# Deformable convolution, attention and 32-expert MLP on one core: three routing groups, two of them inside the last image's steps, and identity products on TensorE

## The chip, the cores and the metric

The kernel runs on one core of a Trainium2 chip. The metric is the device time of one execution in microseconds (us). TensorE (PE) multiplies matrices out of SBUF into PSUM, VectorE (DVE), ScalarE (ACT) and GpSimd (POOL) compute elementwise, and SyncE (SP) issues most of the DMA transfers. Each engine runs its own instructions in order and waits on semaphores.

## The reference

Eight images of 32 x 32 positions with 64 channels go through three stages, each with a residual addition.

```python
x = x + deform_conv(group_norm(x), kernel, bias, offset_w, offset_b)   # 3x3, offsets by a second 3x3 conv
t = to_tokens(x)                                                     # (8, 1024, 64)
t = t + causal_attention(layer_norm(t), Wq, bq, Wk, bk, Wv, bv)        # one head of 64
y = layer_norm(t)
logits = y @ gate_w.T + gate_b                                        # (8, 1024, 32)
probs = softmax(logits, axis=1)                                       # over the tokens
topv, topi = top_k(probs, 8)                                          # each expert takes 8 tokens
pooled = einsum("bked,bke->bed", y[topi], topv)                       # one vector for each image and expert
h = gelu([pooled, 1] @ weight1[e])                                    # 65 x 256, exact gelu
o = [h, 1] @ weight2[e]                                               # 257 x 64
t[topi] += o * topv                                                   # scattered back to the chosen tokens
```

## The kernel before

Tokens stand as 8 tiles of 128 for each image (`tok`). The program has four blocks, with a barrier between each two: `convolve_and_attend`, `route`, `mlp` and `combine`.

**The first block** works through the eight images in a pipeline. For each engine a table (`PE_AT`, `ACT_AT`, `DVE_AT`, `POOL_AT`, `SP_AT`) gives every step of an image a place in the engine's order, and image b is shifted by b times `STEPS`; only the order follows from these numbers, the time is set by semaphores. Images 0, 6 and 7 have tables of their own, images 1 to 5 share one. The steps that matter here:

- *prepare*: PE turns the image to channels (`turn`, L452), ACT and DVE copy it (`raw`, L463, L465), PE sums over groups (`groups`, L503), POOL normalises (`normalise`), PE convolves for the offsets (`offsets`, L553, L560), ACT evicts them (`leave`, L573), DVE and ACT make the interpolation weights ("tents"), which SP writes to DRAM (`near`) and reads back spread over partitions (`stage`, L826; `load`), three pieces deep.
- *convolve*: eight pieces an image. PE multiplies rows with the kernel (`mix`, L1215), ACT copies them (`rows`, L876), ACT finishes the column weights of a piece once its `stage` transfer has landed (`columns`, L866, L869), DVE multiplies weights (`weights`, L1073), PE forms the result in 16 `pair` steps (L1248) and turns it back (`back`).
- *attend*: layer norm, query and key (`query`, `key`), eight score rows with maximum (L1035), exponential (L961), transposes (L1105), values (L1117), output (`out`, L1204), second layer norm, channels (L1125, L914), gate (L1195), and the logits go to ACT's `rows4` (L970) and by four DMAs (L813) to the 128 rows of their half of the images. The choice for the first four images (softmax, top eight, mask in `pm`) runs in DVE steps inside image 7's table (`DVE_CHOICE`).

If some offset is too large, the block's end branches to a slow path (`unless_near`); it isn't taken with these inputs.

**route** asks for the expert weights, makes the choice for images 4 to 7 (`Choice`, L1574 to L1597), and for each half turns the mask (L1662), copies it (L1646) and gathers by 32 products (L1671: for each of 4 images and 8 tiles, two images side by side), which leaves `lhs`. **mlp** does 32 products of layer one (L1704, bias as a 65th row, four experts side by side in the array), gelu, transposes (L1711), layer two (L1719), bias (L1746), a product with a selection matrix that puts results behind their images (L1728), and four copies (L1752). **combine** multiplies with the mask in eight pieces (L1785), adds to the tokens (L1795) and stores each piece by two DMAs (L1777).

## Time and profile before

| | |
|---|---|
| runs | 508.09, 507.71, 504.94 us |
| median | 507.71 us |
| profiled execution | 507.9 us, its span 506.1 us |
| TensorE, busy | 416.1 us (82% of the span) |
| VectorE, busy | 345.3 us (68%) |
| ScalarE, busy | 289.8 us (57%) |
| GpSimd, busy | 159.5 us (32%) |
| mean granted clock of TensorE | 0.897 |
| HBM | 64.74 MB read, 7.01 MB written |

The times are those of whole executions. The busy times are from one profiled execution and overlap each other. A granted clock of 1.00 is 2.4 GHz, 0.50 is 1.2 GHz.

### The profile page before, as it was taken

The page shows a single profiled execution, that of the slowest core. Times are in us where ns is not written, and L with a number is a line of the kernel's source. Part 1 is how long each engine was busy: PE and PEld are TensorE (multiplying, and loading weights), DVE is VectorE, ACT ScalarE, POOL GpSimd, SP SyncE. Part 2 cuts the span into 40 slices and gives each one's busy share as a digit, 9 for nine tenths or more (in the row PEclk, how much of TensorE's full clock was granted, in tenths as well). Part 3 has the DMA queues.
Part 4 walks back from the last instruction along what each step waited for, and adds up shares of the span by engine and source line. Part 5 has one row for each costly group of instructions (what it writes and reads, how often), then busy time and mean ns, then how long its engine had stood idle before and what let it go on. Part 6 is the DMA issues. An engine that isn't in the chain of part 4 may idle for free. (4 is left out here: it accounts for less than half of the span.)

```text
span 506.1 us, 14009 instructions
## 1 busy us (share of the span) xinstructions
PE 416.1 (82%) x5845; PEld 307.5 (61%) x5845; DVE 345.3 (68%) x478; ACT 289.8 (57%) x531; POOL 159.5 (32%) x119
## 2 busy tenths in 40 slices
PE   1606985899999999999999999999999788227574
PEld 0204572576777677767767776767867556226274
DVE  3234668777898889889889989888896653213034
ACT  2323264778787687778677776877676456022100
POOL 2006007106534535472354446040640430310000
PEclk9756597999999999999999999999999969755589
DMA  9598969788787778588867789868730000039208
GB/s 221 97 208 189 222 144 231 179 205 177 188 205 177 177 183 186 123 207 195 186 160 174 175 176 207 198 158 198 181 71 12 2 2 12 1 70 229 84 3 166
DMA packets 33698, 75.61 MB, mean 149 GB/s; under 512 B 22365, under 2 KB 25373, under 8 KB 27293
## 3 DMA queue, kind: packets, MB, share of 16 engines
q1 hardware_dynamic: 28750, 72.68, 62.7%
q10 hardware_dynamic: 4880, 1.98, 1.7%
q8 instruction: 48, 0.79, 0.7%
q14 instruction: 20, 0.16, 0.1%
HBM read 64.74 MB, written 7.01 MB: 142 GB/s over the span
## 5 line engine op out<-in xcount | busy, mean ns | idle before, releaser
L1073 DVE TENSOR_TENSOR wring<-stage 96x640 f32<-96x640 f32 x192 | 173.0, 943 | 32.5 <-ACT stage L869 28.5
L1248 PE MATMUL psum<-wring,zring 96*64 96x160 f32 (+4 forms) x1728 | 124.8, 293 | 6.4 <-DVE wring L1073 6.4
L1248 PEld LDWEIGHTS psum<-wring,zring 96*64 96x64 f32 x1728 | 104.6, 141 | 20.9 <-issue 15.9
L1035 DVE TENSOR_REDUCE negmax<-psum 128x1 f32<-128x128 f32 (+3 forms) x64 | 48.3, 754 | 34.5 <-PE psum L1097 34.4
L1215 PE MATMUL psum<-kern,img 64*32 64x192 f32 x1536 | 58.5, 343 | 9.0 <-ACT zring L876 8.4
L876 ACT ACTIVATE zring<-psum 96x768 f32<-96x768 f32 x64 | 51.4, 803 | 23.0 <-PE psum L1215 21.4
L902 ACT ACTIVATE pT<-psum 128x512 f32<-128x512 f32 (+2 forms) x96 | 46.0, 483 | 28.4 <-PE psum L1105 28.1
L961 ACT ACTIVATE prob<-psum,negmax 128x128 f32<-128x128 f32 (+3 forms) x64 | 47.0, 734 | 22.9 <-DVE negmax L1035 18.4
L1093 PE MATMUL psum<-kT,qT 64*128 64x128 f32 (+4 forms) x400 | 51.7, 361 | 4.6 <-DVE kT L1030 1.5
L1105 PE MATMUL psum<-const,prob 128*128 128x128 f32 x288 | 50.5, 287 | 3.2 <-ACT pT L902 3.0
L866 ACT ACTIVATE stage<-stage,const 96x384 f32<-96x384 f32 x64 | 38.9, 608 | 20.5 <-DMA stage<-near 20.3
L1215 PEld LDWEIGHTS psum<-kern,img 64*32 64x32 f32 x1536 | 29.8, 110 | 25.1 <-ACT zring L876 12.0
L1093 PEld LDWEIGHTS psum<-kT,qT 64*128 64x128 f32 x400 | 33.5, 195 | 18.6 <-issue 9.7
L522 POOL TENSOR_SCALAR gs<-gs 64x1 f32<-64x1 f32 (+1 forms) x8 | 7.4, 927 | 114.1 <-DVE gs L514 114.1
L1117 PE MATMUL psum<-pT,ln 128*64 128x128 f32 x576 | 42.3, 278 | 0.7 <-ACT pT L902 0.7
L1105 PEld LDWEIGHTS psum<-const,prob 128*128 128x128 f32 x288 | 31.9, 144 | 13.8 <-issue 8.0
L1117 PEld LDWEIGHTS psum<-pT,ln 128*64 128x64 f32 x576 | 35.4, 137 | 6.3 <-issue 3.7
L1543 POOL TENSOR_TENSOR rn_tmp<-tok,rn_small 128x512 f32<-128x512 f32 x8 | 11.2, 1402 | 87.4 <-DVE rn_small L1529 87.4
L869 ACT ACTIVATE stage<-stage 96x384 f32<-96x384 f32 x64 | 33.5, 523 | 2.0
L527 POOL TENSOR_SCALAR img<-img,gs 64x1024 f32<-64x1024 f32 x7 | 28.2, 4022 | 0.8
L1543 POOL TENSOR_TENSOR an_tmp<-tok,an_small 128x512 f32<-128x512 f32 x8 | 10.0, 1251 | 47.5 <-DVE an_small L1529 47.5
L582 DVE TENSOR_TENSOR tents<-offT,const 128x1536 f32<-128x1536 f32 x8 | 15.4, 1930 | 9.0 <-ACT offT L573 9.0
(120 smaller groups left out, 525.9 us busy)
## 6 DMA issues: line engine op xcount, KB each, us to landing
stage<-near SPq DMA_DIRECT2D x192, 288.0 KB, 5.5
w<-in_w SPq DMA_DIRECT2D x1, 2080.0 KB
tok<-in_x SPq DMA_DIRECT2D x8, 256.0 KB, 5.2
images<-img SPq DMA_DIRECT2D x8, 256.0 KB, 3.8
w<-in_w SPq DMA_DIRECT2D x1, 2048.0 KB
img<-img SPq DMA_DIRECT2D x7, 256.0 KB, 3.0
near<-tents SPq DMA_DIRECT2D x32, 45.0 KB
shifts<-offT SPq DMA_DIRECT2D x8, 128.0 KB, 6.4
```

The costliest lines, as they stand in the source:

```text
L866: act.activation(dx, dx, ACT.Abs, bias=cst("negx")[0:KX, 0:1]).then_inc(f["abs"], 1)
L869: act.activation(dx, dx, ACT.Relu, bias=1.0, scale=-1.0).then_inc(f["tx"], 1)
L876: act.activation(zring[0:KX, q % ZRING].rearrange("p (s e) f -> p e s f", e=2), psum[0:KX, 0:2, 0:2 * K * C].rearrange("p e (s f) -> p e s ...
L902: act.activation(pT[:, t % DEEP, j * P:(j + nb) * P], psum[:, prob_bank(n, a), 0:nb * P], ACT.Copy).then_inc(s["pe"], 1)
L961: act.activation(prob[:, t % 2, 0:(t + 1) * P].rearrange("p (h k) -> p h k", k=row_half(t)), score_rows(t, a), ACT.Exp, bias=negmax[:, t:t ...
L1035: dve.tensor_reduce(negmax[:, t:t + 1], score_rows(t, a), AX.XY, ALU.max, negate=True).then_inc(s["mx"], 1)
L1073: dve.tensor_tensor(rows[:, ky, :, place], stage[0:KX, q % STG, ky, 1:, :], stage[0:KX, q % STG, ky, 0, :].unsqueeze(1).to_broadcast([KX, ...
L1093: ins = pe.matmul(psum[:, bank, c * n:c * n + n], qT[C * h:C * h + C, t * P:(t + 1) * P], kT[C * h:C * h + C, first:first + n], start=True ...
L1105: ins = pe.transpose(psum[:, prob_bank(n, a), m * P:(m + 1) * P], prob[:, t % 2, (j + m) * P:(j + m + 1) * P], ident)
L1117: ins = pe.matmul(psum[C * h:C * h + C, 7, t // 2 * P:(t // 2 + 1) * P], normed(a)[:, j, :], pT[:, (t + h) % DEEP, j * P:(j + 1) * P], sta ...
L1215: ins = pe.matmul(psum[W * kx:W * kx + W, e, n * K * C:(n + 1) * K * C], img[C * e:C * e + C, b % 2, row, :], kern[C * e:C * e + C, kx, :] ...
L1248: ins = pe.matmul(psum[C * e:C * e + C, 2 + half, (lo % 16) * W:(lo % 16 + n) * W], zring[0:KX, q % ZRING, i % 2 * 2 + e, ky * C:(ky + 1) ...
```

## The change

Everything now stands in one block, `run_all`, without the three barriers. The images form three routing groups, `GROUPS = ((0, 4), (4, 6), (6, 8))`.

- The choice, turning and gathering of groups 0 and 1 (`choose`, `pooled`), and layer one, gelu and transposes of their experts (`many`), are steps in image 7's table. Their SBUF places overlay tiles that the convolution and the attention no longer need: `hidden` and `hiddenT` lie in `pT`, `outs` in `prob`, the third mask in `qT`.
- The expert weights are asked for by a step `weights` in image 7's table on SP, behind the last convolution.
- The last image's logits go directly to their rows of the third group, without a DMA.
- Behind the tables each engine has an end (`pe_end`, `act_end`, `dve_end`), where group 2 (images 6 and 7) gets its choice, gather, experts, weighting and stores, while groups 0 and 1 are moved, weighted and stored in between.
- Layer one takes its bias on DVE (`add_bias`) and puts eight experts side by side, in both halves of the rows. The gather takes one image at a time, with half of the experts on each half of the output rows: 8 tiles x 2 products an image.
- `stay_awake` has PE multiply the identity by itself into a bank that nobody reads: 16 products behind image 0's turn, and 8, 6 and 5 products in `pe_end`.
- All five order tables are new, `STEPS` is 1120.

```diff
-STEPS, ROUND = 944, 4881
+STEPS, ROUND = 1120, 4577
 PE_AT = (      # image 7, the rows that are new
+        pooled=[5889, 6865, 10417, 11042, 13729, 14081],
+        many=[14497, 17361, 17473, 17985, 22001]))
 ACT_AT = (     # image 0
-        columns=[145, 225, 226, 305, 385, 465, 706, 753],
-        rows=[-1583, -287, 81, 257, 497, 705, 737, 929],
+        columns=[-2431, -191, 753, 1185, 1234, 1505, 1729, 1811],
+        rows=[-3535, -1007, -687, 929, 1233, 1521, 1809, 1812],
...
+        if step == 0 and g == 0:
+            pe.wait_ge(f["both"], 2 * B - 1)
+        if step == 0 and g == 1:
+            pe.wait_ge(pooled[0].s_pT, run + 1)
+        if step < 2:
+            pooled[g].turn(pe, step, 2, run)
+        else:
+            pooled[g].gather(pe, 2, run)
...
+        def pe_end(pe):
+
+            many.layer2(pe, 0)
+            stay_awake(pe, 3, 8)
+            many.move(pe, 1)
+            stay_awake(pe, 3, 6)
+            for n in range(3):
+                pe_weigh(pe, n)
+            stay_awake(pe, 3, 5)
+            pooled[2].turn(pe, 0, 0)
+            pe_weigh(pe, 3)
+            pooled[2].gather(pe, 1)
+            for n in range(4, 6):
+                pe_weigh(pe, n)
+            pe.wait_ge(pooled[2].s_pT, 1)
+            single.layer1(pe)
+            for n in range(6, len(strips)):
+                pe_weigh(pe, n)
+            pe.wait_ge(s_x, len(strips))
+            for n in range(4):
+                single.turn(pe, n)
+            single.layer2(pe, 0)
+            single.move(pe, 1)
...
+            act.activation(spare[:, 1:2], ident[:, 0:1], ACT.Exp)
+            choices[2].exponentials(act)
+            act.wait_ge(s_zero, 2)
+            many.keep(act, 1, copy)
+            act.activation(spare[:, 2:3], ident[:, 0:1], ACT.Gelu)
+            pooled[2].keep_turned(act, 0, 0)
+            pooled[2].keep(act, 1)
+            for n in range(4):
+                single.gelu(act, n)
+            for n in (2, 3):
+                single.keep_turned(act, n, copy)
+            store_last(act, 1)
...
+            dve_choose(dve, 2, 0)
+            dve.wait_ge(s["pt"], ONE + B * NCK)
+            many.keep_out(dve, 0)
+            for step in range(1, 5):
+                dve_choose(dve, 2, step)
+            for n in range(len(strips)):
+                dve_add(dve, n)
+            for n in range(4):
+                single.add_bias(dve, n)
+            for n in range(2):
+                single.keep_turned(dve, n, dve.tensor_copy)
+            single.keep_out(dve, 0)
+            single.keep(dve, 1, dve.tensor_copy)
...
+        def stay_awake(pe, bank, count):
+
+            for n in range(count):
+                pe.matmul(psum[:, bank, 0:P], ident, ident, start=True, stop=True)
...
             if n in at["turn"]:
                 bank_free(pe, in_z, b, n, True)
                 prep.to_channels(pe, b)
+                if b == 0:
+                    stay_awake(pe, 7, 16)
...
                 for b, at in in_order(SP_AT):
+                    if at in table(SP_AT, b)["weights"]:
+                        sync.wait_ge(f["mm"], 2 * NG4)
+                        sync.wait_ge(f["w_ok"], K * NG4)
+                        load_weights(sync)
...
+    def gather(self, pe, bank, run=0):
+        half = E // 2
+        pe.wait_ge(self.s_tT, self.parts * (run + 1))
+        for u in range(self.count):
+            for t in range(NT):
+                for r in range(2):
+                    ins = pe.matmul(self.psum[C * r:C * r + C, bank, half * u:half * u + half],
+                                    self.ln2[:, self.first + u, t, :],
+                                    self.taken[:, t, E * u + half * r:E * u + half * r + half],
+                                    start=(t == 0), stop=(t == NT - 1))
+        ins.then_inc(self.s_po, 1)
...
+    def layer1(self, pe, run=0):
+        for i in range(4):
+            for j in range(4):
+                for r in range(2):
+                    ins = pe.matmul(self.psum[E * j:E * j + E, 2 * r + i // 2, i % 2 * HID:(i % 2 + 1) * HID],
+                                    self.lhs[C * r:C * r + C, 4 * i + j, :], self.w1[C * r:C * r + C, 4 * i + j, :],
+                                    start=True, stop=True)
+            if i % 2:
+                ins.then_inc(self.s["h"], 1)
```

ScalarE at the start, from the eviction of image 0's offsets to the raw copy of image 1. `near` to `stage` transfers are what `f_stage0` and `f_stage1` wait for; before:

```order
L573 ACTIVATE offT<-psum,ob 128x256 [waits p_off_mm]
L876 ACTIVATE zring<-psum 96x2x2x192 [waits f_z_mm]
L593 ACTIVATE tents<-tents 128x2x640 [waits p_t_raw]
L596 ACTIVATE tents<-tents 128x2x640 [waits p_t_abs]
L876 ACTIVATE zring<-psum 96x2x2x192 [waits f_z_mm] x2
L463 ACTIVATE img<-psum 64x4x128 [waits p_x_t]
L866 ACTIVATE stage<-stage,const 96x3x128 [waits f_stage0]
```

and now (`memory` holds `stage`, `wring` and `zring`):

```order
L587 ACTIVATE offT<-psum,ob 128x256 [waits p_off_mm]
L607 ACTIVATE tents<-tents 128x2x640 [waits p_t_raw]
L610 ACTIVATE tents<-tents 128x2x640 [waits p_t_abs]
L935 ACTIVATE memory<-psum 96x2x2x192 [waits f_z_mm]
L925 ACTIVATE memory<-memory,const 96x3x128 [waits f_stage0]
L928 ACTIVATE memory<-memory 96x3x128 [waits f_abs]
L935 ACTIVATE memory<-psum 96x2x2x192 [waits f_z_mm] x2
L925 ACTIVATE memory<-memory,const 96x3x128 [waits f_stage1]
L928 ACTIVATE memory<-memory 96x3x128 [waits f_abs]
L477 ACTIVATE img<-psum 64x4x128 [waits p_x_t]
```

The second and third row copies and the raw copy of image 1 moved behind the first and second column steps.

TensorE at the end of the program, from the second group's turn to the move of the results; before:

```order
L1662 MATMUL psum<-const,pm 128x128 [waits r1_tk]
L1671 MATMUL psum<-takenT,ln 64x32 [waits r_tT]
L1615 UNCONDITIONAL_BRANCH
L1698 UNCONDITIONAL_BRANCH [waits barrier_Pool_Activation_PE_DVE_SP_release]
L1704 MATMUL psum<-w,lhs 32x256 [waits s_w]
...
L1719 MATMUL psum<-w,hT 32x64 [waits e_hT]
L1728 MATMUL psum<-outs,pick 128x64 [waits e_out]
```

and now, from the second expert layer of groups 0 and 1 (`ea`) to the first expert layer of group 2 (`r2`, `eb`); L1391 is `stay_awake`, L1224 the weighting:

```order
L2028 MATMUL psum<-memory,pT 32x64 [waits ea_hT]
L1391 MATMUL psum<-const 128x128 x8
L2045 MATMUL psum<-prob,memory 128x64 [waits ea_out]
L1391 MATMUL psum<-const 128x128 x6
L1224 MATMUL psum<-memory,chosen 128x256 [waits c_lg_sb,ea_kept]
L1224 MATMUL psum<-memory,chosen 128x256 x5
L1391 MATMUL psum<-const 128x128 x5
L1936 MATMUL psum<-const,qT 128x64 [waits r2_tT,r2_step]
L1224 MATMUL psum<-memory,chosen 128x256 x2
L1952 MATMUL psum<-memory,ln 64x16 [waits r2_tT]
L1224 MATMUL psum<-memory,chosen 128x128 [waits e_x]
L1980 MATMUL psum<-memory 32x256 [waits r2_pT]
```

Work of groups 0 and 1 moved ahead of and between the steps of group 2.

## Rows read from the trace of the kernel before

**Rows 1.** The page: the span, and TensorE's granted clock in 40 slices

```profile
span 506.1 us, 14009 instructions
...
PEclk9756597999999999999999999999999969755589
```

**Rows 2.** Windows, by stage: length, busy us of each engine, clock, DMA share, GB/s

```profile
100.00:350.00 250.00, 244.70 (x3725) 183.85 (x3725) 219.56 (x298) 188.60 (x351) 104.40 (x70) 1.00 0.79 182
...
390.00:410.00 20.00, 15.37 (x148) 10.93 (x146) 13.34 (x24) 11.00 (x21) 6.53 (x7) 0.98 0.01 2
410.00:420.00 10.00, 9.61 (x54) 7.02 (x52) 4.55 (x6) 4.21 (x12) 4.67 (x5) 0.53 0.01 2
420.00:434.00 14.00, 11.50 (x140) 8.82 (x138) 3.65 (x4) 8.07 (x18) 0.00 (x0) 1.00 0.04 11
434.00:452.00 18.00, 1.77 (x20) 0.98 (x20) 2.99 (x6) 1.07 (x2) 4.96 (x5) 0.57 0.05 11
452.00:474.00 22.00, 11.52 (x148) 10.33 (x152) 5.88 (x7) 5.55 (x9) 2.42 (x3) 0.50 0.78 212
```

**Rows 3.** Timeline, last image: start, length, engine, line, operation, tiles, count

```profile
432.85 1.11 PE L1204 MATMUL psum<-wv,oT 64*128 64x64 f32 x16 [0.69 <-ACT oT L975]
...
443.07 1.09 PE L1125 MATMUL psum<-const,ln 128*128 128x128 f32 x4 [9.11 <-POOL ln L1558]
...
445.71 0.47 ACT L970 ACTIVATE rows<-psum,kbias 128x256 f32<-128x256 f32 x1 [0.92 <-PE psum L1195]
```

**Rows 4.** Timeline of routing, experts and output; the last row is of the windows

```profile
452.19 1.94 PE L1662 MATMUL psum<-const,pm 128*128 128x128 f32 x8 [6.57 <-PEq L1434]
...
455.64 3.63 PE L1671 MATMUL psum<-takenT,ln 128*64 128x32 f32 x64 [1.52 <-ACT takenT L1646]
...
458.29 1.22 DVE L1597 SCALAR_TENSOR_TENSOR pm<-work 128x1024 f32<-128x1024 f32 x1
...
466.32 0.57 ACT L1651 ACTIVATE lhs<-psum 64x64 f32<-64x64 f32 x2 [3.73 <-PE psum L1671]
...
473.64 7.05 PE L1704 MATMUL psum<-w,lhs 65*32 65x256 f32 x64 [7.37 <-DMA pick<-in_pick]
...
484.23 1.99 PE L1719 MATMUL psum<-w,hT 128*32 128x64 f32 x128
...
487.04 3.79 PE L1728 MATMUL psum<-outs,pick 128*128 128x64 f32 x32 [0.81 <-DVE outs L1746]
...
490.86 1.24 DVE L1752 COPY expert_out<-psum 32x128 f32<-32x128 f32 x4 [3.88 <-PE psum L1728]
...
492.63 7.14 PE L1785 MATMUL psum<-expert_out,pm 128*128 128x256 f32 x32 [1.80 <-PEq L1697]
...
499.81 0.69 DVE L1795 TENSOR_TENSOR tok<-psum,tok 128x512 f32<-128x512 f32 x1 [0.17 <-PE psum L1785]
...
505.00:505.50 0.50, 0.00 (x0) 0.00 (x0) 0.00 (x0) 0.00 (x0) 0.00 (x0) 0.50 0.47 100
```

**Rows 5.** Timeline of the start

```profile
5.10 1.09 PE L452 MATMUL psum<-const,tok 128*128 128x128 f32 x4 [5.10 <-DMA tok<-in_x]
...
9.37 0.38 PE L503 MATMUL psum<-mv,const 64*64 64x2 f32 x4 [3.18 <-DVE img L479]
...
13.51 2.73 PE L553 MATMUL psum<-img,ow_pair 128*32 128x256 f32 x24 [3.54 <-DVE img L538]
...
18.43 0.87 PE L1215 MATMUL psum<-kern,img 64*32 64x192 f32 x24 [0.60 <-ACT offT L573]
...
27.13 0.59 ACT L463 ACTIVATE img<-psum 64x512 f32<-64x512 f32 x1 [1.20 <-PE psum L452]
...
31.86 0.61 ACT L866 ACTIVATE stage<-stage,const 96x384 f32<-96x384 f32 x1 [4.14 <-DMA stage<-near]
...
41.19 4.75 PE L1248 MATMUL psum<-wring,zring 96*64 96x128 f32 x36 [2.79 <-DVE wring L1073]
...
48.24 7.33 SPq L826 DMA_DIRECT2D stage<-near  x9
```

1094 lines of the change are left out of this document (616 added, 478 removed).

## Prediction, made before the run

> **What bounds the kernel now.** The profiled execution took 507.9 us, its span is 506.1 [rows 1], so 1.8 us lie around the span; the median of the three runs is 507.71, 0.2 less. I read the page first: the row of the granted clock shows a long flat middle at 9 and a head and a tail at 5 and 6. The table of windows then splits the span [rows 2]. From 100 to 350 us TensorE is busy 244.70 of 250 us at clock 1.00: that part is bound by TensorE, and no order of the same products makes it shorter. From 434 to 474 us it is busy 13.3 of 40 us, at clock 0.57 and 0.50: that part is a chain of short steps with waits in between. The change works there.
>
> The timeline of the tail gives the steps. The last image's attention leaves TensorE at 432.85+1.11 = 433.96; normalising takes until the transposes at 443.07, and the logits are out of PSUM at 445.71+0.47 = 446.18 [rows 3]. The routing block starts only at 452.19: 6.0 us go to the copy of the logits through DMA, its landing, the branch and the barrier. The choice of the second half ends at 458.29+1.22 = 459.51. Two gathers and their copies last until 466.32+0.57 = 466.89. Then the first product of the experts waits until 473.64, 7.37 us of it for the DMA of the weights, which is asked for at the start of the routing block. Expert layers, move and copies last until 492.10, the weighting until 499.77, and the stores keep the DMA queues full until past 505 [rows 4].
>
> **The tail, step by step.** I take durations at half clock as half as long where the step runs at 2.4 GHz.
>
> Last attention. The first two groups' turning and gathering move into it. Their cost on TensorE: eight transposes, 1.94 at half clock, so 1.0; the gather of four images, now 64 products of the same 64-column loads in place of 32, 2 x 3.63 / 2 = 3.6; and the turning of the second group, 1.0. Together 5.6 us before the last output product. TensorE's idle time from 410 to 434 is 2.9 us (24 less 9.61 less 11.50), so 2.7 are left over if all of it is filled. Against that, the query's copy now stands ahead of the previous image's output copy, and the first score may start up to 2 us earlier; and from 410 to 420 the clock was 0.53, a loss of some 4.8 us that a fuller engine might not have. Bounds -4 and +6; I take +1.5, near the sum of fill and early score, since nothing shows that the clock will hold: 435.5.
>
> From there to the logits it is 12.2 us now (433.96 to 446.18). VectorE gets five steps of the experts between the two sums of the norm, and TensorE three turns; they fit into GpSimd's time (VectorE is busy 2.99 of 18 us). What does not fit is the fourth turn ahead of the gate, a copy by ScalarE, and a logits copy twice as long: I take 1.3. Logits at 449.0. No DMA follows, nor a barrier: the 6.0 us go, of which about 1 returns as TensorE's own branch.
>
> The order of TensorE's end matters now. VectorE needs 7.3 us for a choice (from the block's begin, 452.19, to 459.51) and lets one addition of 0.69 in: ready at 449.0 + 0.5 + 7.3 = 456.8. But TensorE has queued ahead of the last group's turn: the second expert layer, 1.99; eight identity products, 1.9 (a product with 128-column weights takes 3.79/16 = 0.24); the move, 16 products, half of them with 64 columns, 2.9; the wait for six copies by ScalarE (0.3 each, as 1.24/4 on VectorE), 1.7, in which six identity products fit; three pieces of weighting at 7.14/8 = 0.89, 2.7; and five identity products, 1.2. From 449.0 that is 12.4: the turn starts at 461.4, 4.6 us after VectorE is ready. So **the identity products and the weighting ahead of the turn are the late party**, not the choice.
>
> From 461.4: turn 1.0, copy 0.7, gather of two images 1.8, copy 0.4. Layer one follows with 32 products on eight corners of the array instead of four: half of the 7.05 for the corners and half again for the clock, 1.8 (3.5 if the corners bring nothing). I take the first, since L1215, on six corners, does 12 products of 192 columns in 0.87 us [rows 5], and at L1704's pace on four they would take 12 x 0.083 = 0.99. Two pieces of weighting 0.9 and the last addition 0.5 stand before VectorE's first bias: 468.5. Four biases at 0.69 and a gap, 2.9; the last gelu, the last turn and two copies, each of 512 columns and about as long, 2.75; layer two 2.0, addition 0.8, move of eight narrow products 1.0, copies 0.7, weighting 1.8, addition 0.75: 481.2. The last stores carry half a megabyte instead of two; now the last addition ends at 500.50 and the queues empty by about 505.3 [rows 4], 4.8 us under a full queue. I take 3.9, and 0.7 to the end: **span 486**, 20 below 506.1. The weights cost nothing: they are asked for behind the last image's convolution, about where the stretch from 390 with a DMA share of 0.01 begins [rows 2], and what took from 452 to 473 is there before 415. If that cover went, 7 us would return.
>
> **The middle.** The tables of all engines are new, but their step lists agree but for neighbours that change places. With 98% of TensorE's time taken, I give it nothing: between -2 and +3 us.
>
> **The start.** It is costed apart, because here the change adds. At 5.10 the first transposes take 1.09, the slow pace, which is half clock if the four records scale as L1662's eight do at 1.94 [rows 4, 5]; L553, at 13.51, takes 2.73 for its 24 records, and by 18.43 the pace is full: L1215 has its 0.87 [rows 5]. Sixteen identity products are queued at 6.2, ahead of the group sums that are due at 9.37. At half clock they take 16 x 0.47 = 7.6 us and end at 13.8, at full clock 3.8 and 10.0; I take 11.0, since the pace came up within the work that began at 13.51 as well. Group sums about 1.4 us later; after them TensorE stands idle 3.5 us as before, so the offsets gain only if the clock is kept through that. Bounds -0.4 (held) and +4 (never up); I take +1.4.
>
> Second, ScalarE's row copies 1 and 2 of the first image now stand behind the first column step, which waits for the stage DMA until 31.86. TensorE's third mix, the turn of image 1 and its raw copy (27.13 before) hang on them: they come at about 37. The raw copy goes from before the weights of piece 1 to between them on VectorE, so the first pair, 41.19 before, starts some 2.5 us later, and image 1's normalise, which the SP queue waits for ahead of the next nine stage loads (48.24 before), 3 to 4 later. TensorE fills part with pair 2 to 4 and two mixes moved ahead of the offsets of image 1. From this I take +1.6, between 0 and 4. Start together: **+3**. After 100 us TensorE has no slack in which a late start could be won back.
>
> Sum: 506.1 - 20 + 3 = 489.1, and 1.8 around it: **491 us**.
>
> **A rule weighed.** TensorE's rows first: it went to 0.50 after the idle stretch from 434 on and stayed there through 452 to 474 although busy for half of it [rows 2]; the products L1662 and L1704 show the doubled durations. The Trainium skill says in "TensorE: Matmul & The Clock Gate", part on the HAM clock gate, that the clock is halved when the engine has been idle and returns after sustained activity, whatever the products are for. The trace agrees with the fall. By that rule the end is the 486 summed above; if the fillers do nothing for the clock, it is rival 1's. At the start it would grant the rise, and its loss again in the idle stretch behind the group sums.
>
> **Rivals.**
> 1. *The clock falls all the same* in the last attention or the end. Three of the four fillers are each under 2 us, and from 410 to 420 the engine was busy 9.61 of 10 us and yet at 0.53 [rows 2]. Half clock from 449 to 468 doubles layer two, fillers, move, weighting, turn, gather: about 10 us, less what hid waits; with half of the stretch struck +6: 497 us. Against it: from 390 to 410 it was busy 15.4 of 20 us and kept 0.98.
> 2. *TensorE is not late at the turn.* If attention gains from a held clock (-3) and the start costs nothing (-3), and the queue ahead of the turn is shorter by 1: 484 us. For it: the idle 2.9 us and the early score; against it: the fillers stand in a fixed row.
> 3. *Slower than before.* The new tables put a wait into each of the repeating images: for instance ScalarE's row copies behind column steps, so that a pair finds its rows late. TensorE has no slack there, so every microsecond counts six times. It decides from (506.1 - 489.1)/6 = 2.8 us per image on: at 3.5 it is 512 us. Against it: the steady rows differ by neighbours only, and TensorE's idle time is now 5.3 us in 250.
> 4. *The branch or the order makes the end serial*: if the choice waits for TensorE's layer two through VectorE's one addition, and biases wait for all eight additions, each by 2 us more than I have: 496 us, inside rival 1's time.
>
> **How the numbers follow.** Forecast as summed 0.5; rival 1 with 4, 0.3, at 496 to 501; rival 2 0.15, at 482 to 486; rival 3 0.03; the rest 0.02 lies lower. The range 482 to 500 leaves out the slow end of rival 1, rival 3 and the lowest. About 1% is what a measurement of this kernel tells from no change: faster than 502.6 has 0.95, within 1% 0.03, slower 0.02.
>
> **What would show it.** In the profile after: no idle stretch between logits and choice above 1.5 us; the weights' DMA over before 415; the turn of the last group starting at 461 + 3 with TensorE busy right up to it, while VectorE's choice was ready some 4 us earlier (if TensorE waits for VectorE there, that step is wrong); first group sums after 10.5; the first pair near 45; the end at 489. I am wrong if the stretch from 100 to 390 has another length by over 3 us, or if the clock row shows a 5 between 440 and 480.

## The result, and the profile after

Over 20 runs each, the changed kernel took 501.65 us at the median (497.22 to 509.31) and the kernel before 511.21 (504.45 to 515.94): a ratio of 0.985, interval 0.982 to 0.988. It is faster by 1.5%; the forecast was 491.0. The profiled execution shown first is one of the changed kernel's longer ones, 507.41 us; a second profile of the same kernel (run e1_same below, span 499.4) stands for the median where sizes are given.

The page and the table of windows of the changed kernel, answering to [rows 1, 2] (the columns are those of rows 2):

```profile
span 505.5 us, 14907 instructions
...
PEclk9655988859999999999999999999999999788897
```

```profile
80.00:100.00 20.00, 14.48 (x199) 8.48 (x189) 18.57 (x22) 11.36 (x20) 10.29 (x7) 0.87 0.81 187
100.00:120.00 20.00, 20.00 (x218) 14.63 (x218) 10.20 (x15) 10.46 (x21) 0.00 (x0) 0.62 0.76 181
...
400.00:413.00 13.00, 10.52 (x96) 7.13 (x96) 6.95 (x12) 7.87 (x16) 7.82 (x8) 1.00 0.98 413
...
434.00:452.00 18.00, 17.30 (x301) 15.45 (x306) 3.47 (x8) 6.90 (x16) 2.06 (x2) 0.75 0.01 2
452.00:474.00 22.00, 14.21 (x215) 11.08 (x200) 9.99 (x14) 7.91 (x12) 2.91 (x4) 0.82 0.02 4
```

From 434 to 452 TensorE is now busy 17.30 of 18 us, where it was 1.77 (a part of that is the last attention itself, whose last output product starts at 445.92 and not at 432.85), and the weights come at 400 to 413 with the DMA queues full (0.98), under the last attention. What was not forecast: from 100 to 120 it is busy every microsecond and yet has a clock of 0.62.

The timeline of the start, answering to [rows 5]:

```profile
6.14 5.30 PE L1391 MATMUL psum<-const 128*128 128x128 f32 x32
11.38 0.29 PE L517 MATMUL psum<-mv,const 64*64 64x2 f32 x4
15.34 1.90 PE L567 MATMUL psum<-img,ow_pair 128*32 128x256 f32 x24 [3.56 <-DVE img L552]
20.49 1.52 PE L1492 MATMUL psum<-kern,img 64*32 64x192 f32 x24 [0.59 <-ACT offT L587]
...
33.80 0.61 ACT L925 ACTIVATE memory<-memory,const 96x384 f32<-96x384 f32 x1 [8.27 <-DMA memory<-near]
39.33 0.59 ACT L477 ACTIVATE img<-psum 64x512 f32<-64x512 f32 x1
44.21 3.15 PE L1525 MATMUL psum<-memory 96*64 96x128 f32 x24 [1.32 <-DVE memory L1332]
```

And its end, answering to [rows 3, 4] (L1475 the gate, L1041 the logits, L2028 layer two, L1391 the products with the identity, L2045 the move, L1224 and L1280 the weighting, L1936 the last group's turn, L1980 its layer one):

```profile
445.92 1.11 PE L1461 MATMUL psum<-wv,oT 64*128 64x64 f32 x16 [0.30 <-ACT oT L1036]
457.54 1.05 PE L1475 MATMUL psum<-channels,gate 64*32 64x512 f32 x4
458.63 1.10 ACT L1041 ACTIVATE logits<-psum,kbias 32x1024 f32<-32x1024 f32 x1 [0.58 <-PE psum L1475]
462.14 1.28 ACT L1289 ACT_TABLE_LOAD   x1 [2.40 <-issue]
462.21 0.42 PE L2028 MATMUL psum<-memory,pT 128*32 128x64 f32 x14 [3.62 <-issue]
465.39 3.36 PE L2028 MATMUL psum<-memory,pT 128*32 128x64 f32 x114 [2.75 <-issue]
468.85 0.69 DVE L2035 TENSOR_TENSOR prob<-psum,memory 128x512 f32<-128x512 f32 x1 [7.82 <-PE psum L2028]
472.99 1.22 DVE L1915 SCALAR_TENSOR_TENSOR qT<-memory 64x1024 f32<-64x1024 f32 x1
475.81 2.86 PE L1224 MATMUL psum<-memory,chosen 128*128 128x256 f32 x12
478.51 1.28 PE L1391 MATMUL psum<-const 128*128 128x128 f32 x10
479.72 0.71 PE L1936 MATMUL psum<-const,qT 64*128 64x64 f32 x8
484.48 1.96 PE L1980 MATMUL psum<-memory 64*32 64x256 f32 x64
493.19 3.64 PE L2028 MATMUL psum<-memory,pT 128*32 128x64 f32 x128 [0.89 <-ACT pT L1287]
501.43 0.69 DVE L1321 TENSOR_TENSOR tok<-psum,tok 128x512 f32<-128x512 f32 x1 [0.20 <-PE psum L1280]
```

Two idle stretches stand between logits and last layer two, 3.62 and 2.75 us, and their releaser is "issue": TensorE waits for nothing that the profile shows. ScalarE has one of 2.40 at the same place. This place is the branch over the slow path. VectorE waits 7.82 us there for TensorE's layer two, because its order puts the addition that follows layer two (L2035) between the first step of the last choice and the others.

Checkpoints, each the start of an instruction, split the span. "Tokens 1" is the addition of the second image's convolution to its tokens, "tokens 7" that of the last image, "out" the last output product, "gate" the last gate. The two columns on the right are lengths. "Forecast" is worked out from the prediction's terms, with the gate put 2.2 us ahead of the end of the logits' copy, as it is in the profile after (457.54 and 459.73).

| kernel | tokens 1 | tokens 7 | out | gate | gate to end | span |
|---|---|---|---|---|---|---|
| before | 121.47 | 390.73 | 432.85 | 444.93 | 61.2 | 506.1 |
| forecast | 124.5 | 393.7 | 437.4 | 449.8 | 39.3 | 489.1 |
| changed, first profile | 132.54 | 400.50 | 445.92 | 457.54 | 48.0 | 505.5 |
| changed again (e1_same) | 130.37 | 398.32 | 442.12 | 454.21 | 45.2 | 499.4 |

Against the forecast the median-like execution is 10.3 us long: 4.6 before the last attention, 0.1 in it, -0.3 from there to the gate, and 5.9 behind it. So the two questions are what costs 6 us behind the gate, and what costs 5 in the start.

### The profile page after: what moved, and what is told of

Same layout as the page of the kernel before. It is cut to its first block, busy times and chain, and to the rows that moved or that the text cites. A ratio compares the mean times of both kernels' runs of the same rounds, so it can differ in the third digit from the quotient of the medians.

```text
span 505.5 us, 14907 instructions
## 1 busy us (share of the span) xinstructions
PE 434.1 (86%) x6279; PEld 325.2 (64%) x6279; DVE 359.7 (71%) x494; ACT 302.4 (60%) x554; POOL 166.7 (33%) x118
## 4 chain that ended last, share of the span: by engine, by line
PE 55%; DVE 15%; DMA 9%; POOL 6%; issue 6%; ACT 5%; SPq 3%; POOLq 0%; DVEq 0%; ACTq 0%
PE psum L1525 15%; DMA memory<-near 7%; PE psum L1352 6%; PE psum L1492 5%; PE psum L1364 5%; DVE memory L1332 5%; PE psum L1376 5%; POOL img L541 2%; PE psum L1391 2%; PE psum L2028 1%; PE psum L574 1%; PE psum L567 1%; SPq L881 1%; PE psum L1356 1%; PE psum L1440 1%
## 5 line engine op out<-in xcount | busy, mean ns | idle before, releaser
L1332 DVE TENSOR_TENSOR memory<-memory 96x640 f32<-96x640 f32 x192 | 176.4, 963 | 25.6 <-ACT memory L928 24.8
L1525 PE MATMUL psum<-memory 96*64 96x160 f32 (+4 forms) x1728 | 130.8, 299 | 7.1 <-DVE memory L1332 4.5
L1525 PEld LDWEIGHTS psum<-memory 96*64 96x64 f32 x1728 | 107.2, 144 | 27.3 <-issue 25.4
L1492 PE MATMUL psum<-kern,img 64*32 64x192 f32 x1536 | 59.6, 348 | 16.6 <-ACT memory L935 16.0
L935 ACT ACTIVATE memory<-psum 96x768 f32<-96x768 f32 x64 | 51.2, 800 | 25.0 <-PE psum L1492 23.0
L925 ACT ACTIVATE memory<-memory,const 96x384 f32<-96x384 f32 x64 | 38.9, 608 | 24.7 <-DMA memory<-near 24.6
L1352 PEld LDWEIGHTS psum<-kT,qT 64*128 64x128 f32 x400 | 32.7, 191 | 18.6 <-issue 11.6
L536 POOL TENSOR_SCALAR gs<-gs 64x1 f32<-64x1 f32 (+1 forms) x8 | 5.9, 738 | 116.9 <-DVE gs L528 116.9
L1376 PEld LDWEIGHTS psum<-pT,ln 128*64 128x64 f32 x576 | 36.8, 139 | 5.5 <-issue 2.7
L1856 POOL TENSOR_TENSOR rn_tmp<-tok,rn_small 128x512 f32<-128x512 f32 x8 | 11.6, 1449 | 83.6 <-DVE rn_small L1842 83.6
L928 ACT ACTIVATE memory<-memory 96x384 f32<-96x384 f32 x64 | 33.5, 523 | 2.0
L541 POOL TENSOR_SCALAR img<-img,gs 64x1024 f32<-64x1024 f32 x7 | 30.6, 4366 | 0.8
## 6 DMA issues: line engine op xcount, KB each, us to landing
memory<-in_w SPq DMA_DIRECT2D x2, 2048.0 KB, 10.3
```

The lines of the kernel that those rows point to most:

```text
L541: pool.tensor_scalar(self.rows(b), self.rows(b), gs[:, 0:1], gs[:, 4:5], ALU.subtract, ALU.mult).then_inc(self.s["pn"], 1)
L925: act.activation(dx, dx, ACT.Abs, bias=cst("negx")[0:KX, 0:1]).then_inc(f["abs"], 1)
L935: act.activation(zring[0:KX, q % ZRING].rearrange("p (s e) f -> p e s f", e=2), psum[0:KX, 0:2, 0:2 * K * C].rearrange("p e (s f) -> p e s ...
L1332: dve.tensor_tensor(rows[:, ky, :, place], stage[0:KX, q % STG, ky, 1:, :], stage[0:KX, q % STG, ky, 0, :].unsqueeze(1).to_broadcast([KX, ...
L1352: ins = pe.matmul(psum[:, bank, c * n:c * n + n], qT[C * h:C * h + C, t * P:(t + 1) * P], kT[C * h:C * h + C, first:first + n], start=True ...
L1376: ins = pe.matmul(psum[C * h:C * h + C, 7, t // 2 * P:(t // 2 + 1) * P], normed(a)[:, j, :], pT[:, (t + h) % DEEP, j * P:(j + 1) * P], sta ...
```

## The experiments

The kernels ran in four groups of four, each in five rounds beside the kernel before, and each group on a chip of its own. The median of the kernel before was 510.94 us in the group of e1, e2, e4 and e5, 508.87 in that of e3, e6, e7 and b1, 509.98 in that of e8, e10, c1 and c2, and 511.58 in that of the d runs. Medians are compared directly inside a group only; across groups the ratio to the kernel before is the better measure, and it too can be off by about 1% (see d3_tail_unfilled). "Gate to end" is read from one profile of each kernel.

**e1_same**, no edit. 

> The changed kernel unchanged, for a second profile. In the first profile of it the convolution of the last image ended at 400.5 us in place of 390.7, and 9.4 of those 9.8 us arose between the tokens of image 0 and image 1, where the granted clock was 0.50 from about 98 to 115 us. If that stretch is a matter of this execution, the second profile has the last image's tokens 5 us or more earlier or has its slow stretch elsewhere, and a span of 496 to 500; if the new order makes it, the tokens of image 1 come at 130 to 134 us again. The gap between the logits of the last image (ScalarE until 459.7) and the second expert layer (whole from 465.4) should repeat within 1 us either way. Time 0.985 of the kernel before.


Measured 501.96 us, ratio 0.983 (0.979 to 0.987). Tokens 1 came at 130.37, where the expectation put it if the new order made the slow stretch; but three other profiles of kernels with the same instructions up to there have it at 125 (below), so the order alone does not make it. From the logits to the whole of layer two it is 5.1 us again (456.40 to 461.52; 5.7 in the first profile).

**e2_no_start_fill.**

```diff
-                if b == 0:
-                    stay_awake(pe, 7, 16)
```

> The changed kernel without the 16 identity products behind the first image's turn. My theory: they delay the group sums of image 0 from 9.4 to 11.4 us and buy nothing, since the offsets ran at the slow pace behind them all the same; then the first stage transfers land 2 us earlier and the time is 2 us (0.4%) lower than that of the unchanged copy. Rival: they shift when the clock rises and falls later in the start, where TensorE was at 1.00 from 50 to 63 us with them and at 0.61 without; then the time is equal or 2 to 4 us higher.


Measured 499.08 us, ratio 0.978 (0.974 to 0.982). The 16 products at the start are no help but cost up to 3 us; the intervals overlap a little.

**e4_old_order**: the tables of all engines list the steps in the order of the kernel before up to the last image's query and key, and in the new order from there on; nothing else differs. 

> The changed kernel with the order of the kernel before on all five engines up to the last image's query and key; behind that the new order, the new end, the early weights, the three groups, all as changed. Theory A, the new tables cost time in the middle or in the start: the last image's tokens come at 391 to 394 us and the time is 6 to 10 us below the unchanged copy. Theory B, only the executions differ by where the clock falls: it is within 2 us of the unchanged copy. With the 16 products of the start still in, the group sums are at 11.4.


Measured 502.10 us, ratio 0.981 (0.976 to 0.986): no difference. In the times the new order of start and middle is neither gain nor loss. (Its profile has tokens 1 at 124.83, 5.5 us ahead of e1_same, and gives 3.5 back behind the gate, where its stops are 4.81 and 2.84 us.)

**e5_no_branch**: the slow path, the load of its flag and the branch left out (with these inputs the slow path is never taken).

```diff
-            large = load_flag(eng)
-            with eng.If(large < 1):
-                eng.nop()
-            with eng.Else():
-                again(eng)
```

> The changed kernel without the slow path for large offsets: no load of the flag, no branch over it, no code of it (it isn't taken with these inputs). Theory: after the branch the engines wait for instructions, TensorE 3.6 us before the second expert layer and 2.8 more within it, ScalarE 2.4; without it the second layer runs right behind the gate's product and ends some 6 us earlier, and the time falls by 5 to 6 us. Rival: the wait there is for the logits and VectorE's choice, or the code is fetched late in any case; then under 1 us is gained.


Measured 493.28 us, ratio 0.966 (0.961 to 0.971); gate to end 39.05 us against 45.2. This is the largest gain of any edit to the changed kernel, and the 39.05 is what the prediction's sum gives from gate to end (39.3). Of the 10.4 us between the two profiles (span 489.0 against 499.4) 6.15 stand behind the gate; the other 4.3 stand ahead of it (5.2 at tokens 1) and are not the branch's doing.

**b1_before_no_branch**: the same edit in the kernel before. 

> The kernel before with the slow path, its flag and its branch left out (the slow path's work is never asked for with these inputs). It tells whether the branch cost the kernel before the same. The idle time between the logits and the routing block was 6.0 us there, of which the copy of the logits through DMA hides some 2 to 4: if the code behind the jump is what is late, 507 to 509 against 511.0 for the kernel before; if the branch was hidden behind the DMA of the logits, 510.5 to 511.


Measured 507.1 us, ratio 1.000 (0.997 to 1.003). The idle time between the last gate and the routing block fell from 6.57 to 4.89 us, and the whole did not move measurably. So, by one profile of each, the branch cost about 1.7 us there, beside the copy through DMA: that is why it looked cheap.

**e10_short_jump**: flag load, test and jump stay, but the body jumped over is one empty instruction.

```diff
             with eng.Else():
-                again(eng)
+                eng.nop()
```

> The changed kernel with flag load, test and jump kept, and the slow path behind the test cut to one empty instruction, so that the jump over it is a few instructions long. If what costs is the length of the jump (code far behind the test has not been fetched), TensorE's last layer two starts within 2 us of the logits' copy and the whole is 493 to 496. If every jump that is taken costs some microseconds, whatever its length, it is 500 to 502, as the changed kernel. If part of it is the flag load and the test, 496 to 499.


Measured 494.23 us, ratio 0.972 (0.965 to 0.978), gate to end 39.4. It tells the jump's length from the jump itself: a jump over one instruction costs next to nothing, one over the slow path (840 instructions on TensorE in the built program, 264 on ScalarE) costs 6 us. The DMA view of e1_same from 440 to 470 us shows code being fetched there (queue, packets, MB, share):

```profile
q8 instruction: 5, 0.08, 1.0%
q14 instruction: 3, 0.02, 0.3%
```

In the same 30 us of e10_short_jump and e5_no_branch q8 has 4 and 3 packets and q14 none, so more code is fetched where the long jump is taken.

The timelines of TensorE at this place, first e1_same, then e10_short_jump:

```profile
458.59 0.65 PE L2028 MATMUL psum<-memory,pT 128*32 128x64 f32 x14 [3.33 <-issue]
...
461.52 3.07 PE L2028 MATMUL psum<-memory,pT 128*32 128x64 f32 x114 [2.28 <-issue]
```

```profile
453.33 1.86 PE L2028 MATMUL psum<-memory,pT 128*32 128x64 f32 x115 [0.37 <-issue]
456.53 0.42 PE L2028 MATMUL psum<-memory,pT 128*32 128x64 f32 x13 [1.34 <-issue]
```

The first stop shrinks from 3.33 to 0.37 us, the second from 2.28 to 1.34; the second is there without any branch as well (e5_no_branch: 1.35). That the stop is the fetch is not shown directly: no row ties a packet to the instruction that waits. The packets of queue q8 are 0.08 MB / 5 = 16 KB each, those of q14 smaller. The Trainium skill gives in "Advanced Engine Details and Errata", part on the ISA cache, a cache line of 16 KB, 256 instructions; the packets of q8 agree, and a jump over 840 instructions then always leaves the line. Under control flow timing the same page gives about 51 ns for a branch and 108 ns for a compare with branch: e10's 0.37 us does not speak against that at a near target, e1's 3.33 does at a far one, and there the measurement decides.

The stop costs once more through the clock (columns as in rows 2), e1_same and then e10_short_jump:

```profile
455.00:465.00 10.00, 4.39 (x134) 3.80 (x133) 1.51 (x2) 3.72 (x5) 0.00 (x0) 0.66 0.02 7
465.00:475.00 10.00, 9.98 (x83) 9.22 (x82) 6.99 (x10) 2.77 (x8) 0.00 (x0) 1.00 0.13 28
```

```profile
455.00:465.00 10.00, 8.64 (x92) 7.88 (x83) 6.15 (x9) 4.51 (x12) 0.00 (x0) 1.00 0.01 2
465.00:475.00 10.00, 10.00 (x172) 8.22 (x170) 3.49 (x7) 0.80 (x2) 0.00 (x0) 1.00 0.64 133
```

**e6_fall_through**: the branch kept, but every engine's end stands inside it, right behind the test, and a second time behind the slow path.

```diff
             with eng.If(large < 1):
-                eng.nop()
+                end(eng)
             with eng.Else():
                 again(eng)
+                end(eng)
```

> The changed kernel with its branch kept, but the end of every engine written twice, once inside the body that runs when the offsets are small, right behind the test, and once behind the slow path. It tells what of the 8.7 us that leaving the slow path out gave belongs to the jump over the slow path's code, and what to the test itself (flag load and compare). If it is the jump over a large body into code that nobody has fetched (my reading), then the end runs as without a branch: gate to end 39 to 41 us, whole 494 to 496. If it is the test, whatever the place of the code, then 500 to 502, as the changed kernel. If every taken branch costs the same, the cost moves behind the end, since the body's last instruction must jump over the second copy: then about 498.


Measured 496.87 us, ratio 0.980 (0.975 to 0.985), gate to end 41.4. It computes all that the changed kernel does, slow path included, and is 4 to 5 us faster than the two neighbours of its group (e3, e7: 501.0 and 501.4); by the ratios the gap is smaller, and the intervals overlap. With e5 and e10 the direction is settled. Up to the turn of the last group it runs as e10 does (15.3 us behind the gate in both); nearly all of its 2.0 us more stand behind the last store's issue, 4.2 us to the end against 2.3. There the usual path has to jump over the second copy, and from 470 to 500 us q14 has 5 packets of instructions where e10 has none; that this jump is the 2 us is likely and not shown. The issue lines, e6_fall_through and then e10_short_jump (spans 490.1 and 491.3):

```profile
484.86 1.06 ACTq L1250 DMA_DIRECT2D out<-tok  x2
```

```profile
487.99 0.99 ACTq L1250 DMA_DIRECT2D out<-tok  x2
```

**e3_no_end_fill**: the changed kernel without its products of the end.

```diff
-            stay_awake(pe, 3, 8)
             many.move(pe, 1)
-            stay_awake(pe, 3, 6)
             for n in range(3):
                 pe_weigh(pe, n)
-            stay_awake(pe, 3, 5)
```

> The changed kernel without the 8, 6 and 5 products with the identity in the last group's end (the 16 at the start stay). Two theories. (a) The clock in the end is held by the work itself, and the products only stand ahead of the last group's turn: then the turn starts some 2 us earlier than in the changed kernel and the whole is 500 us, about 2 below the changed kernel run again (502.0). (b) The products keep the clock: without them it falls to 0.50 between the choice and the last stores, the last layer two and the weighting take twice as long, and the whole is 504 to 508.


Measured 500.99 us, ratio 0.986 (0.980 to 0.991): no difference. In its profile the two stops are 5.12 and 2.46 us, 2 longer together than in e1_same, and gate to end is 45.4. The clock is low behind the jump with or without the products: 0.50 from 460 to 465 us here, 0.59 there.

**d3_tail_unfilled**: the same edit, made to e6_fall_through. 

> The version with the end inside the branch and its order unchanged, without the 8, 6 and 5 products of the end. If these products hold the clock, it falls to 0.50 for some 20 us behind the choice and the whole is 500 to 503, as in the reordered end without them. If they only stand in the queue, the turn of the last group comes 2 us earlier and the whole is 494.5 to 495.5. (In the changed kernel itself leaving them out moved the whole by less than 1 us: 501.0.)


Measured 497.17 us, ratio 0.967 (0.960 to 0.973). The median is that of e6 (496.87), and the ratio is 1.3% lower than e6's (0.980); the two ran in different groups, and that is how far such comparisons can be trusted. In its profile the clock is 0.50 from 460 to 465 and 0.54 from 465 to 470, the move takes 4.66 us in place of 2.97 and three pieces of weighting 5.34 in place of 2.86; the products' own time is saved and the clock's time lost, gate to end 43.2 against 41.4. Neither expected value held, and the times do not tell the two kernels apart.

**c1_tail**: e6_fall_through without the products and with another order of the end. VectorE's first two biases move ahead of its last five additions, the other two ahead of its last four.

```diff
             many.layer2(pe, 0)
-            stay_awake(pe, 3, 8)
             many.move(pe, 1)
-            stay_awake(pe, 3, 6)
-            for n in range(3):
-                pe_weigh(pe, n)
-            stay_awake(pe, 3, 5)
+            pe_weigh(pe, 0)
             pooled[2].turn(pe, 0, 0)
-            pe_weigh(pe, 3)
+            pe_weigh(pe, 1)
             pooled[2].gather(pe, 1)
-            for n in range(4, 6):
-                pe_weigh(pe, n)
+            pe_weigh(pe, 2)
             pe.wait_ge(pooled[2].s_pT, 1)
             single.layer1(pe)
-            for n in range(6, len(strips)):
+            for n in range(3, len(strips)):
                 pe_weigh(pe, n)
...
```

> The changed kernel with the end written inside the branch, right behind the test, and with another order of that end: none of the 8, 6 and 5 products; on TensorE the turn of the last group behind one piece of weighting in place of three, layer one behind three pieces in place of six, the other five behind layer one; on VectorE the biases ahead of the last five additions. The choice is ready some 10.5 us after the gate and is no more waited for by TensorE's queue: the turn starts 11 to 12 us after the gate in place of 15.3, the end comes 37 us after the gate in place of 41.4, and the whole is 492 to 494 against 496.9 for the version with the end inside the branch. If the products keep the clock up in the end, it falls to 0.50 between choice and last layer two and the gain is eaten: 496 to 499.


Measured 502.60 us, ratio 0.983 (0.976 to 0.991): a miss. The turn comes 11.6 us after the gate as meant, but the end 44.9 us after it.

**d2_tail_filled**: the same order, with products in its two gaps.

```diff
             many.layer2(pe, 0)
+            stay_awake(pe, 3, 5)
             many.move(pe, 1)
+            stay_awake(pe, 3, 6)
             pe_weigh(pe, 0)
```

> The reordered end (turn of the last group behind one piece of weighting) with 5 products with the identity back between layer two and move and 6 between move and weighting. If they hold the clock, the gather of the last group takes 2.0 us in place of 3.9, layer one 2.0 in place of 3.3, and the end comes 37.5 to 39 us after the gate in place of 44.9: whole 493 to 495. If the clock falls behind the gate whatever TensorE does there, it is 501 to 503, as without them.


Measured 493.16 us, ratio 0.965 (0.960 to 0.970). The 9.4 us between the two medians (1.8% by the ratios) come from different groups and are not all the products': of the 14.4 us between the two profiles 8.6 stand ahead of the gate, where the instructions are the same, and 5.8 behind it (44.9 against 39.0). The windows of both (c1_tail above, d2_tail_filled below):

```profile
450.00:460.00 10.00, 8.17 (x102) 4.84 (x101) 5.34 (x10) 4.42 (x8) 4.97 (x5) 0.83 0.01 2
460.00:482.00 22.00, 19.34 (x301) 14.98 (x308) 9.26 (x13) 7.33 (x16) 0.00 (x0) 0.61 0.17 36
```

```profile
450.00:460.00 10.00, 8.42 (x184) 6.93 (x183) 5.81 (x8) 5.14 (x10) 0.00 (x0) 1.00 0.01 3
460.00:482.00 22.00, 18.60 (x341) 15.15 (x340) 9.69 (x18) 6.63 (x14) 0.00 (x0) 0.92 0.35 74
```

and one line of each timeline, the first piece of weighting, at half and at full clock:

```profile
468.59 2.07 PE L1224 MATMUL psum<-memory,chosen 128*128 128x256 f32 x4 [1.56 <-ACT memory L1290]
```

```profile
460.83 1.13 PE L1224 MATMUL psum<-memory,chosen 128*128 128x256 f32 x4
```

In c1_tail TensorE stands idle 1.10 us before the move and 1.56 us behind it; the clock falls at about 465, behind the first gap and still within the move, and stays at 0.50 until about 482, although TensorE is busy 19.34 of the 22 us. In d2_tail_filled the same two gaps are filled and gate to end is 39.0. Both ends were profiled twice: c2_all (below) has c1's end and again 0.50 from 465 to 480 us and 44.9 from gate to end, d4_tail_and_start (below) has d2's and 36.8. So products that nobody reads did hold the clock here, where they stood in the waits and no longer stop followed.

**e7_act_start**: on ScalarE alone, row copies 1 and 2 and the raw copy of image 1 ahead of the first column step, as before. The steps of ScalarE in a row (image.step):

```diff
+0.rows1, 0.rows2, 1.raw0
 0.columns0
-0.rows1, 0.rows2
 0.columns1
-1.raw0
 0.columns2
```

> The changed kernel with three steps moved on ScalarE alone: the first image's row copies 1 and 2 and the raw copy of image 1 stand ahead of the first column step, as in the kernel before. If the late start is ScalarE's order (the prediction gave it 1.6 us), image 1's raw copy comes at 27 to 29 us in place of 39 and the whole is 500.4. If the late start is TensorE's clock and its order alone, the raw copy comes early and the whole stays within 0.5 us of the changed kernel (502.0).


Measured 501.35 us, ratio 0.987 (0.983 to 0.991): no difference. ScalarE's raw copy came at 33.06 in place of 39, later than meant, and VectorE's half of it at 38.93 as ever: the first pair stayed at 44.86. The edit missed its aim.

**e8_old_start**: the start of every engine in the old order, the rest new, with the 16 products. 

> The changed kernel with the start of every engine in the order of the kernel before, up to the first pairs of image 1, and the order of the changed kernel from there on; the 16 products at the start stay. It isolates what the prediction called the second part of the start and gave 1.6 us. If the order of the start costs that, image 1's raw copy comes at 27 to 29 us, the first pair at 42 to 43 and the whole is 499 to 500.5. If only the 16 products and the clock behind them matter, the first pair comes early all the same, the clock gives the lead away before 130 us, and the whole is 501 to 502.


Measured 509.90 us, ratio 1.001 (0.997 to 1.006): a miss, 8 us (by the ratios 1.8%) slower than the changed kernel. ScalarE's raw copy came at 30.67 and the first pair at 44.91, so with the 16 products the old order brought no early pair at all.

**c2_all**: c1_tail with the old start and without the 16 products. 

> The version before with the 16 products at the start left out and the start of every engine in the order of the kernel before. If the three causes add (branch 5 to 8, end's queue 4, start 3 to 4.5), the whole is 487 to 490. If the lead of the start is lost again in the middle, 491 to 493.


Measured 498.77 us, ratio 0.981 (0.974 to 0.988), above both expected ranges. Its raw copy came at 27.16 and its first pair at 41.35, just as in the kernel before, yet image 1's tokens came at 132.24 (136.68 in e8). From 80 to 120 us e8_old_start has clock 0.57 and 0.66, c2_all 0.57 and 0.91, e5_no_branch 0.91 and 1.00 (in this order), and in the first two TensorE also stands idle between 100 and 120, 2.25 and 2.03 us:

```profile
80.00:100.00 20.00, 15.79 (x151) 8.11 (x140) 14.22 (x16) 6.60 (x11) 7.70 (x6) 0.57 0.73 167
100.00:120.00 20.00, 17.75 (x205) 12.73 (x205) 8.25 (x13) 11.80 (x24) 0.00 (x0) 0.66 0.62 142
```

```profile
80.00:100.00 20.00, 15.79 (x140) 8.27 (x140) 14.25 (x16) 7.29 (x14) 7.70 (x6) 0.57 0.74 172
100.00:120.00 20.00, 17.97 (x267) 13.25 (x269) 12.09 (x18) 13.94 (x28) 0.00 (x0) 0.91 0.73 166
```

```profile
80.00:100.00 20.00, 14.14 (x207) 8.34 (x197) 18.93 (x23) 11.97 (x21) 10.70 (x7) 0.91 0.84 192
100.00:120.00 20.00, 20.00 (x311) 15.63 (x309) 15.69 (x25) 14.58 (x29) 2.89 (x3) 1.00 0.94 212
```

The lead of c2's early first pair is gone by tokens 0 (77.84; e2_no_start_fill, with its first pair at 42.32, has 77.92), and the loss comes behind it.

**d1_no_start_fill**: e6_fall_through with the edit of e2_no_start_fill. 

> The version with the end inside the branch, without the 16 products at the start. Without them the changed kernel was 2.9 us faster (499.1 against 502.0). If that gain is one of the start alone, it adds here: 493 to 494.5 against 496.9. If the start gives back by its clock what it wins (image 1's tokens at 124 to 125 us with and without them in the two fastest profiles), it is 496 to 497.5.


Measured 495.65 us, ratio 0.969 (0.964 to 0.974), 1.2 below e6. **d4_tail_and_start**: d2_tail_filled with it. 

> The reordered end with its 5 and 6 products, and without the 16 products at the start. If both gains are real, 490 to 492; if the products of the end do not hold the clock, 498 to 500; if the start gives its gain back, 493 to 495.


Measured 489.22 us, ratio 0.956 (0.950 to 0.962), 3.9 below d2 in the same group. Leaving the 16 out gave 2.9, 1.2 and 3.9 us in three pairs (by the ratios 0.5, 1.1 and 0.9%); each is near its uncertainty, all have one sign. Where the gain arises is not shown: tokens 1 is 5.8 us earlier without them in the first pair of profiles, but 5.0 and 2.3 later in the other two. In the third pair the end is 2.2 us shorter (36.8 against 39.0), and layer two has lost the stop of 1.45 us that it has in d2. d4_tail_and_start computes everything, slow path included, and is the fastest version: 4.4% under the kernel before, where the change has 1.5%.

## Why the prediction was wrong

The direction was right and the size was not: -16.7 us forecast, -9.6 measured between the medians, and 501.65 lies outside the range of 482 to 500.

**The step that failed** is "the 6.0 us go, of which about 1 returns as TensorE's own branch". The branch had no row of its own in the trace before, and I took what the DMA of the logits left over. With that DMA gone, the jump over the slow path stands on the path alone: stops of 3.33 and 2.28 us on TensorE, 2.38 on ScalarE, and a stretch at half clock behind them. Together 6 us (45.2 less 39.05 or 39.4) on top of the sum, which had let layer two begin about 1 us behind the gate's product, with the logits out, and had nothing else for the branch. The stop delays VectorE too: it lets the one addition in, as the prediction says, but the sum that gives 456.8 has no wait for it, and in e1_same it waits 6.99 us for layer two (1.66 in e10_short_jump).

**The rest of the end added up.** Without the far jump gate to end measured 39.05 and 39.4 us against 39.3. The late party at the last group's turn was TensorE's queue, as said: in the changed kernel the choice was ready at 472.99 + 1.22 = 474.21 and the turn started at 479.72, 5.5 us later, where 4.6 were forecast; without the branch it is 4.8. Group two's layer one on eight corners took 1.96 (1.8 forecast). The weights were in by 413 (415). But the turn came at 479.7 and not at 464, and between logits and choice stand idle stretches of 3.62 and 2.75 us where the prediction allowed none above 1.5: these two signs say wrong, at just this place. Turning earlier, as this reading suggests, and with the waits filled, took another 2.4 us from gate to end (e6 to d2, 41.4 to 39.0).

**The second miss is a fall of the clock between 80 and 120 us, which the sum put at nothing.** The parts of the start came near the forecast: group sums at 11.38 (11.0), ScalarE's raw copy late (39.33; 37), the first pair at 44.21 (near 45). The prediction made +3 of it. At tokens 0 (the first image's addition) the changed kernel is 1.7 and 2.6 us behind the kernel before in its two profiles, at tokens 1 it is 11 and 9. Nine profiles are of kernels with the same instructions up to there, and they are from 3.4 (e6) to 12.5 us (c1) behind at tokens 1. Five of them stand within half a microsecond at tokens 0 (79.1 to 79.6), and yet three have tokens 1 at about 125 (e5, e6, d2: 3.4 to 3.8 behind, near the +3), e3 has it at 129.28 and the first profile of the changed kernel at 132.54. What differs is the clock: 0.62 from 100 to 120 us in the first profile, 1.00 in e5's. Busy throughout at 0.62 is a loss of about 0.38 x 20 = 7.6 us (an estimate), most of the 9.4 that arise between tokens 0 and 1. I had taken the 100 us mark for the end of the start, since the kernel before had full clock from there [rows 2], and rival 1 looked for a fallen clock in the last attention and the end alone. The kernel before may have had luck too, since its median here lies 3 us above its profiled execution.

The 16 products were priced at 1.4 and cost 1 to 4. They did not bring the pace that they were meant for: the first mix comes at 20.49 and takes 1.52 us, where it came at 18.43 and took 0.87. The order was priced at 1.6, and its experiments (e4, e7) show nothing in the times, while the old start before the new middle is 8 slower (e8).

**The middle** was right: from tokens 1 to tokens 7 it takes 268.0 us in both profiles against 269.3. The last attention was priced at +1.5 and got 3.3 and 1.7; from there to the gate nothing was added, where 0.3 was forecast up to the gate.

**The rivals.** The time is just above that of the first, a fallen clock. It did fall, near the place named (449 to 468), but mostly as a consequence: the stop behind the jump came first (e1_same: 0.73 from 455 to 460 and 0.59 from 460 to 465), and without the jump the clock held through the choice (e10: 1.00 from 455 to 475). Ahead of the jump it dips as well, to 0.66 from 450 to 455 in e1_same. Rival 4 names a part of the mechanism: the choice did wait for TensorE's layer two through VectorE's one addition, because of the stop. Rival 3 did not come, the middle being 1.3 us shorter, and nor did rival 2: TensorE's queue was the late party. The sign that the prediction gave for a fallen clock, a 5 in the clock's row from 440 to 480, did not show, because a slice of 12.6 us averages over it. The Trainium skill's rule in "TensorE: Matmul & The Clock Gate", part on the HAM clock gate, says that activity releases the throttle. c1_tail and d2_tail_filled agree that filled waits keep the clock; the stretches of 20.00 of 20 us busy at 0.62 (100 to 120) and 19.34 of 22 at 0.61 (c1_tail, 460 to 482) show that being busy did not at once bring it back.

**What stays open** is why the clock falls between 80 and 120 us in some executions and versions and not in others. The experiments changed order and filling there and found effects from -4 to +8 us, but none isolates the condition, and one profile for each kernel is too few for it. So the 4.6 us ahead of the last attention have a cause that is read from the clock's rows and not shown by an experiment.

## What to carry to other kernels

A branch over a body that is never run costs little as long as a DMA or another engine's wait covers it; when a change takes that cover away, price the jump (here a stop of 3.3 to 5.1 us and a second one behind it), and put the usual path right behind the test, or make the body short. The version with the usual path behind the test still shows 2 us more behind its end. Idle products hold the clock where they fit into a wait, and only cost where work is queued behind them: fill the gaps of a chain that is already in the right order, and turn first what the slower engine has ready. An early lead in a stretch that runs at an unsteady clock is not a gain until the trace shows it at the next checkpoint. One profile is one execution: the same instructions took 45.6 us (e5, tokens 0 to tokens 1) and 53.0 us (first profile of the changed kernel) between two checkpoints here, so look at a second profile before a difference is put down to the edit.

## What the runs showed of the hardware

- A taken jump over the slow path (840 instructions in the built program) stopped TensorE for 3.33 us (3.62 in the first profile, up to 5.12 in e3_no_end_fill), one over a single instruction for 0.37.
- Straight code stops as well: 1.35 us in the middle of layer two in e5_no_branch, which has no branch. It does not in every version: c1_tail, d1_no_start_fill and d4_tail_and_start run the 128 records of that layer in one piece of 1.99 us.
- TensorE's clock was 0.62 in the mean from 100 to 120 us of the changed kernel, in which the engine was busy 20.00 of 20 us; in e5_no_branch it was 1.00 there, with the same instructions up to that point.
- Two gaps of 1.10 and 1.56 us, with work between them, went with 17 us at half clock (c1_tail, 465 to 482, from behind the first gap on); with 5 and 6 products in them (d2_tail_filled) the clock was 1.00 up to 470.
